# A fused decoder layer on one core: the output projection of five token tiles moved from the mixer into the attention, by way of DRAM

## What is computed

```python
# block 1, the mixer: a state space layer on layernorm(x)
zxbcdt = x @ W_in.T                      # z 1024, xBC 1280, dt 64 columns
xBC = silu(causal_conv(xBC)); dt = softplus(dt_raw + dt_bias)
M = (C @ B.T) * exp(cum_i - cum_j) * dt  # per head, chunks of 128 tokens
y = M @ xs + exp(cum) * C @ S_prev + D * xs
yz = y * silu(z)
yn = yz * rsqrt(mean(yz * yz) + EPS) * norm_w
x = x + yn @ W_out.T                     # 1024 -> 512, the output projection
# block 2: softmax attention of layernorm(x) over the context, 32 query heads, 8 kv heads of 16
# block 3: the two best of 8 gated experts for each token
```

## Time and profile before

| | |
|---|---|
| median of 3 runs | 1400.34 us (1399.75 to 1400.81) |
| the profiled execution's own time | 1394.34 us |
| its span, first to last instruction | 1392.4 us |
| mean granted TensorE clock | 0.977 of full |
| busy share PE, PEld, DVE, ACT, POOL | 92, 53, 59, 51, 42% |
| instructions | 23244 |

### The profile page before, as it was taken

The page is one execution under the profiler, slowest core; times in us unless marked ns, Lnnn a source line. Parts: engine busy times, 40 slices in busy tenths (PEclk is TensorE's granted clock), DMA queues, the critical chain, the costliest instruction groups (busy, mean ns, idle before and its releaser), DMA issues.

```text
span 1392.4 us, 23244 instructions
## 1 busy us (share of the span) xinstructions
PE 1286.9 (92%) x7783; PEld 739.6 (53%) x7783; DVE 822.8 (59%) x1840; ACT 705.9 (51%) x1350; POOL 580.8 (42%) x871
## 2 busy tenths in 40 slices
PE   6799999999999999888888888889999999999996
PEld 4567777767676767553334334234444444444443
DVE  5898888787878778578988898661111111111111
ACT  2767676777767666744778767641111111111110
POOL 1465556665656556672333334341222222222221
PEclk9999999999999999987999999989999999999999
DMA  9000000000000000002001010023344344344222
GB/s 351 24 8 5 8 6 9 5 8 5 8 6 8 5 4 9 9 1 102 13 28 44 32 32 33 32 77 106 77 137 136 58 133 143 80 103 136 46 46 31
DMA packets 40354, 73.41 MB, mean 53 GB/s; under 512 B 18544, under 2 KB 22896, under 8 KB 39216
## 3 DMA queue, kind: packets, MB, share of 16 engines
q1 hardware_dynamic: 30304, 48.49, 10.0%
q0 software_dynamic: 8736, 20.61, 7.9%
q10 hardware_dynamic: 1200, 2.82, 0.5%
HBM read 149.30 MB, written 19.99 MB: 122 GB/s over the span
## 4 chain that ended last, share of the span: by engine, by line
PE 66%; DVE 18%; issue 6%; ACT 5%; POOL 3%; DMA 1%; SPq 1%; POOLq 0%; DVEq 0%; ACTq 0%
PE work_ps L572 12%; PE gate_ps L1573 10%; PE up_ps L1573 10%; PE down_ps L1557 9%; PE work_ps L644 7%; PE work_ps L577 4%; DVE maxes L1263 3%; DVE conv L771 3%; PE work_ps L1089 3%; PE mturn_ps L577 2%; DVE decay L767 2%; PE work_ps L664 2%; PE work_ps L1080 2%; ACT prob L1161 1%; PE work_ps L652 1%
## 5 line engine op out<-in xcount | busy, mean ns | idle before, releaser
L572 PE MATMUL work_ps<-xnT,w_in 128*128 128x256 f32 (+1 forms) x1216 | 289.1, 386 | 4.3 <-DVE xdt L902 2.4
L572 PEld LDWEIGHTS work_ps<-xnT,w_in 128*128 128x128 f32 (+1 forms) x1216 | 226.8, 193 | 54.8 <-issue 21.9
L767 POOL TENSOR_TENSOR decay<-decay,cbm 128x512 f32<-128x512 f32 x128 | 183.8, 1437 | 147.4 <-ACT decay L762 144.3
L1661 POOL DMA_INDIRECT out_dram<-y_out,ids x39 | 61.9, 1587 | 334.3 <-DVE row_w L1625 228.7
L1263 DVE TENSOR_REDUCE maxes<-work_ps 128x2 f32<-128x512 f32 x256 | 166.0, 681 | 28.7 <-PE work_ps L1065 27.7
L1161 ACT ACTIVATE prob<-work_ps 128x512 f32<-128x512 f32 x256 | 142.3, 609 | 66.2 <-PE work_ps L1080 65.6
L1640 DVE TENSOR_TENSOR act<-gelu,up_ps 128x512 f32<-128x512 f32 x39 | 26.8, 688 | 251.8 <-PE up_ps L1573 251.8
L762 ACT ACTIVATE decay<-decay 128x512 f32<-128x512 f32 x256 | 162.1, 640 | 12.5 <-DVE xnT L1212 5.4
L758 ACT ACTIVATE decay<-work_ps 128x512 f32<-128x512 f32 x256 | 138.7, 600 | 38.4 <-PE work_ps L652 37.8
L1573 PE MATMUL gate_ps<-w_e,xgT 128*128 x312 | 140.5, 593 | 1.4 <-ACT xgT L1590 1.0
L1557 PE MATMUL down_ps<-w_e,actT 128*128 x312 | 140.4, 593 | 0.8 <-ACT actT L1603 0.8
(11 more groups left out here) (271 smaller groups left out, 1947.7 us busy)
## 6 DMA issues: line engine op xcount, KB each, us to landing
w_e<-c_experts_dram SPq DMA_DIRECT2D x39, 3072.0 KB
normed_tokens<-r_xn SPq DMA_DIRECT2D x17, 256.0 KB, 2.2
out_dram<-x_sb SPq DMA_DIRECT2D x17, 256.0 KB, 2.5
x_sb<-x_dram SPq DMA_DIRECT2D x1, 3072.0 KB, 17.4
w_in<-c_w_inT_dram ACTq DMA_DIRECT2D x1, 2560.0 KB, 11.8
w_in<-c_w_inT_dram SPq DMA_DIRECT2D x1, 2048.0 KB, 9.7
w_out<-c_w_outT_dram SPq DMA_DIRECT2D x1, 2048.0 KB, 22.5
RT<-cum_scratch SPq DMA_DIRECT2D x32, 48.0 KB
```

Source lines behind the costliest of these rows:

```text
L572: m = e.matmul(ps[0:width, at:at + L], w_in[:, k, col:col + width], xnT[b % 2][:, k, :], start=(k == 0), stop=(k == KD - 1))
L767: return e.tensor_tensor(four(decay[s % NDECAY]), four(decay[s % NDECAY]), cb, ALU.mult)
```

## The change

LATE names tiles 7, 9, 11, 13 and 15, the second tiles of sequences 3 to 7. For these the mixer makes the gated rows and their sum of squares, root included, as before, but in place of `out` and `x_add` SyncE stores the rows (512 KB) to DRAM (`yz_out`, slot f + 9), and the rows' buffer is free once the store has landed. In the attention SyncE loads them back (`yz_in`) and TensorE does `out` in 8 parts of one matmul (two records): tile 7 at items 1, 3, ... 15 with x_add at 17, its load in slot -1 behind `mixed` and `n_out(0, 1)` of slot -2; tile 9 at items 25, 28, ... 46 with x_add at 48, its load at item 20; the others 32 items later each. `yz_in` of tile 9 to 15 waits for `out` of the tile before in the list. Late `out` takes one of the five shared banks from its first part to x_add.

The rows of roots are kept per tile (y_rows for rstats). `mixed` waits for `rstat` of the last tile. The query statistics of sequences 0 and 1 stay together; those of 2 to 7 are made one sequence at a time, two `q_bn` at items 2 and 3 of each 32, `q_stats` at 4, `q_newton` at 5. The small routing tables are loaded at item 2 as before, the first expert's weights at item 162, after `out` of tile 15. The buffers of w_out, yz and some small ones change places in memory, so that w_out and yz stay alive in the attention.

The diff, without the lines that only change a buffer's place:

```diff
@@ -42,6 +42,8 @@
 BANKS = 8
+LATE = [TPB * b + 1 for b in range(3, NB)]
+OUT_PARTS = lambda tile: 8 if tile in LATE else 4
 DT_COL, X_COL = HID, HID + NH
@@ -140,7 +142,10 @@
             put(f + 13, ("rms_newton", tile))
-            for part in range(4):
+            if tile in LATE:
+                put(f + 9, ("yz_out", tile))
+                continue
+            for part in range(OUT_PARTS(tile)):
                 put(f + 9 + part, ("out", tile, part))
@@ -186,7 +191,7 @@
     return slots
-DMA_ONLY = {"freed", "mixed", "cum_out", "cum_in", "ctx_in", "n_out", "router_in", "first_expert", "r_store", "out_in", "c_weight_out", "keep_warm", "warm"}
+DMA_ONLY = {"yz_out", "yz_in", "freed", "mixed", "cum_out", "cum_in", "ctx_in", "n_out", "router_in", "routing_in", "first_expert", "r_store", "out_in", "c_weight_out", "keep_warm", "warm"}
 
@@ -230,6 +235,8 @@
     def allowed(stage, *key):
+        if stage == "out" and key[0] in LATE:
+            return range(5)
         if stage == "score":
@@ -262,11 +269,11 @@
             put(r - 12, ("ctx_in", b))
-        if b and b % 2 == 0:
-            for t in range(2 * TPB):
-                put(r + t, ("q_bn", b * TPB + t))
-            put(r + 4, ("q_stats", b // 2))
-            put(r + 5, *[("q_newton", b // 2, i) for i in range(3)])
+        if b >= 2:
+            for t in range(TPB):
+                put(r + 2 + t, ("q_bn", b * TPB + t))
+            put(r + 4, ("q_stats", b))
+            put(r + 5, *[("q_newton", b, i) for i in range(3)])
         for t in range(TPB):
@@ -286,7 +293,8 @@
         if b == 1:
-            put(2, ("first_expert",))
+            put(2, ("routing_in",))
+            put(n * 5 + 2, ("first_expert",))
         for g in range(4):
@@ -305,6 +313,12 @@
             put(f + 20 + late + 2 * t, ("r_keep", b, t))
+    for m, tile in enumerate(LATE):
+        at, step = (n * m - 7, 3) if m else (1, 2)
+        put(at - 5 if m else -1, ("yz_in", tile))
+        for part in range(OUT_PARTS(tile)):
+            put(at + step * part, ("out", tile, part))
+        put(at + step * 7 + 2, ("x_add", tile))
     for g, at in enumerate((4 * n + 20, 7 * n, 7 * n + 27)):
@@ -355,6 +369,7 @@
     tokens = nc.dram_tensor("normed_tokens", [(NT + 1) * P, DIM + NE], F32).ap()
+    yz_dram = nc.dram_tensor("yz_scratch", [len(LATE), P, HID], F32).ap()
     cum_dram = [nc.dram_tensor(f"cum_scratch{i}", [3, NH, TPB, P], BF16).ap() for i in range(2)]
@@ -379,6 +394,7 @@
         store_weights = semaphore("store_weights")
+        store_yz, load_yz = semaphore("store_yz"), semaphore("load_yz")
         load_e = [semaphore(f"load_e{i}") for i in range(WR)]
@@ -395,6 +411,7 @@
         a_rows = sb(top, "a_rows", [P, 4, NT])
+        y_rows = sb(top, "y_rows", [P, 4, NT])
         xnT = [sb(top, "xnT0", [P, KD, L])]
@@ -405,9 +422,12 @@
...
+            yz = [sb(st, f"yz{i}", [P, NCZ, P]) for i in range(2)]
...
@@ -637,10 +654,14 @@
                 if part == 0:
-                    e.wait_ge(*done("yz", tile // TPB, tile % TPB, 1))
+                    if tile in LATE:
+                        e.wait_ge(load_yz, 16 * (LATE.index(tile) + 1))
+                    else:
+                        e.wait_ge(*done("yz", tile // TPB, tile % TPB, 1))
                     if tile == 0:
                         e.wait_ge(*done("scale_out"))
-                for ct in (2 * part, 2 * part + 1):
+                each = NCZ // OUT_PARTS(tile)
+                for ct in range(each * part, each * (part + 1)):
                     m = e.matmul(work(stage, tile)[:, :], yz[tile % 2][:, ct, :], w_out[:, ct, :], start=(ct == 0), stop=(ct == NCZ - 1))
@@ -914,27 +935,31 @@
                 if tile >= 2 and hf == 0:
-                    e.wait_ge(*done("out", tile - 2, 3))
+                    if tile - 2 in LATE:
+                        e.wait_ge(store_yz, 16 * (LATE.index(tile - 2) + 1))
+                    else:
+                        e.wait_ge(*done("out", tile - 2, OUT_PARTS(tile - 2) - 1))
                 own.settle(e.tensor_tensor(y, four(dx), four(work("y", b, c, hf)), ALU.add))
...
                 e.wait_ge(*done("ones", b, c, hf))
+                now = slice(b * TPB + c, b * TPB + c + 1)
                 if hf == 0:
-                    e.tensor_copy(rstats[:, 3:4], work("ones", b, c, hf)[:, 0:1]).then_inc(piece_done[stage], 1)
+                    e.tensor_copy(y_rows[:, 3, now], work("ones", b, c, hf)[:, 0:1]).then_inc(piece_done[stage], 1)
                 else:
-                    e.tensor_tensor(rstats[:, 0:1], work("ones", b, c, hf)[:, 0:1], rstats[:, 3:4], ALU.add).then_inc(piece_done[stage], 1)
+                    e.tensor_tensor(y_rows[:, 0, now], work("ones", b, c, hf)[:, 0:1], y_rows[:, 3, now], ALU.add).then_inc(piece_done[stage], 1)
             elif stage == "rms":
...
                 e.wait_ge(*done("rstat", tile // TPB, tile % TPB, 1))
-                own.settle(e.tensor_scalar(rstats[:, 0:1], rstats[:, 0:1], 0.25 / HID, RMS_EPS, ALU.mult, ALU.add))
-                root_guess(e, own, rstats[:, 0:1], rstats[:, 1:2], rstats[:, 2:3]).then_inc(piece_done[stage], 1)
+                own.settle(e.tensor_scalar(y_rows[:, 0, tile:tile + 1], y_rows[:, 0, tile:tile + 1], 0.25 / HID, RMS_EPS, ALU.mult, ALU.add))
+                root_guess(e, own, *[y_rows[:, i, tile:tile + 1] for i in range(3)]).then_inc(piece_done[stage], 1)
             elif stage == "x_add":
...
                 e.wait_ge(*done("rms_newton", tile))
-                e.wait_ge(*done("out", tile, 3))
-                e.scalar_tensor_tensor(x_sb[:, tile, :], work("out", tile)[:, :], rstats[:, 1:2], x_sb[:, tile, :], ALU.mult, ALU.add).then_inc(piece_done[stage], 1)
+                e.wait_ge(*done("out", tile, OUT_PARTS(tile) - 1))
+                e.scalar_tensor_tensor(x_sb[:, tile, :], work("out", tile)[:, :], y_rows[:, 1, tile:tile + 1], x_sb[:, tile, :], ALU.mult, ALU.add).then_inc(piece_done[stage], 1)
             elif stage == "mix_v":
@@ -981,7 +1006,7 @@
                 e.wait_ge(*done("rms", *key))
-                root_newton(e, own, rstats[:, 0:1], rstats[:, 1:2], rstats[:, 2:3]).then_inc(piece_done[stage], 1)
+                root_newton(e, own, *[y_rows[:, i, key[0]:key[0] + 1] for i in range(3)]).then_inc(piece_done[stage], 1)
 
@@ -1023,6 +1048,11 @@
 
+            elif stage == "yz_out":
+                tile, = key
+                e.wait_ge(*done("yz", tile // TPB, tile % TPB, 1))
+                e.dma_start(yz_dram[LATE.index(tile), :, :], yz[tile % 2][:, :, :].rearrange("p c j -> p (c j)")).then_inc(store_yz, 16)
+
         def repeated(e, bank, count):
@@ -1040,7 +1070,7 @@
             elif stage == "mixed":
-                e.wait_ge(*done("x_add", NT - 1))
+                e.wait_ge(*done("rstat", *last_unit))
             elif stage == "k_turn":
@@ -1135,7 +1165,7 @@
                 tile = b * TPB + t
-                e.wait_ge(*done("q_newton", b // 2, 2))
+                e.wait_ge(*done("q_newton", b if b >= 2 else 0, 2))
                 if b:
@@ -1234,15 +1264,16 @@
                 tile, = key
-                if tile >= 2 * TPB and tile % (2 * TPB) == 0:
-                    e.wait_ge(*done("q_stats", tile // (2 * TPB) - 1))
+                if tile >= 2 * TPB and tile % TPB == 0:
+                    e.wait_ge(*done("q_stats", tile // TPB - 2 if tile >= 4 * TPB else 0))
+                if tile in LATE:
+                    e.wait_ge(*done("x_add", tile))
                 e.bn_stats(a_bn[:, tile % (2 * TPB), :], x_sb[:, tile, :]).then_inc(piece_done[stage], 1)
             elif stage == "q_stats":
-                j, = key
-                ts = slice(2 * TPB * j, 2 * TPB * (j + 1))
+                ts = queried(*key)
                 e.wait_ge(*done("q_bn", ts.stop - 1))
-                for t in range(2 * TPB):
-                    m = e.bn_aggr(a_mv[:, ts.start + t, :], a_bn[:, t, :])
+                for t in range(ts.start, ts.stop):
+                    m = e.bn_aggr(a_mv[:, t, :], a_bn[:, t % (2 * TPB), :])
                 own.settle(m)
@@ -1401,6 +1432,9 @@
 
+        def queried(j):
+            return slice(TPB * j, TPB * (j + 1)) if j else slice(0, 2 * TPB)
+
         def placed_in(t):
@@ -1423,10 +1457,10 @@
             elif stage == "mixed":
-                e.wait_ge(*done("x_add", NT - 1))
+                e.wait_ge(*done("rstat", *last_unit))
             elif stage == "q_newton":
                 j, step = key
-                ts = slice(2 * TPB * j, 2 * TPB * (j + 1))
+                ts = queried(j)
                 e.wait_ge(*(done("q_newton", j, step - 1) if step else done("q_stats", j)))
@@ -1492,11 +1526,19 @@
                 e.wait_ge(load_ctx, 16 * (b + 1))
-            elif stage == "first_expert":
+            elif stage == "yz_in":
+                tile, = key
+                e.wait_ge(store_yz, 16 * len(LATE))
+                if tile - 2 in LATE:
+                    e.wait_ge(*done("out", tile - 2, OUT_PARTS(tile - 2) - 1))
```

(6 more changed lines are left out.)

13 lines of the change are left out of this document (6 added, 7 removed).

## The result

The changed kernel takes 1411.45 us (median of 8 runs, 1404.91 to 1414.71), the kernel before 1400.03 in the same comparison (8 runs). The ratio is **1.0087, 95% interval 1.0064 to 1.0109**: 12 us slower, where 4 us faster was forecast, and 1.4 us above the range given.

The account below looks back on a forecast made before the run. TensorE, busy 92%, nearly fills the mixer; in the attention no engine is full and they wait in turns. Mixer -18.1, first scores net 0, start +5, tiles 9 to 15 +9: -4.1, so 1396 us against 1400.34, range 1382 to 1410.

Parts of the forecast that it names:

- Mixer, 18.1: Mixer batches of tiles 7 to 13: 20.1 us gained without the late projection, less 2 for the clock, so 18.1.
- x_add and its wait and the 0.90 go: 4.1 us: Steady mixer, tiles 7 and 9: VectorE loses x_add, its wait and a z gate wait, 4.1 us gained per tile.
- The mixer's end, 6: Mixer's end, tile 15: without its groups VectorE's queue decides and the first score comes 6 us earlier.
- the 6 gained are waited away: Attention's start: tile 7's rows load in 3.3 us and later work queues behind, so the net gain is 0.
- The start, 5: Attention's first items, to item 16: tile 7's parts and half clock cost 0.6 to 5.6 us, 5 taken.
- Tiles 9 to 15, 9: Attention items 25 to 142: four tiles' parts cost 9 us, between TensorE's own sum of 5.9 and full exposure of 27.6.
- a part fits behind two waiting scores: Attention, tiles 9 to 15: a part of 0.86 us fits there, the reason for taking 9 us, near the low end.
- they go with the uncertainty of the 9: Query statistics by batch: three more small chains, 0.5 us on VectorE and 3.3 on POOL, given no cost of their own.
- SyncE's wait for yz holds only transfers due ten slots later: Mixer's yz stores: SyncE's wait for yz delays nothing needed soon, so it costs nothing.
- B: Rival: the attention absorbs the parts, 0 to 5.9 in place of 9; 11.6 to 27 us faster, 1373 to 1389; chance 0.18.
- D: Rival: with four shared banks left, TensorE's waits for folds double, 23 in place of 9; 1410 us, slower; chance 0.25.
- C: Rival: the attention's start eats the rest, half clock through item 24, 9 in place of 5; 1400 us, no change; chance 0.19.

Follow-up runs that it names:

- floor: Changed kernel without the late tiles' projection: no matmuls, bank, yz load or x_add; yz stores and statistics by batch stay; 1384.27 us, 0.9892 against the kernel before.
- the run with three late tiles: Kernel before with only tiles 11, 13 and 15 projected among the attention's items, tile 15 from its own buffer, statistics in twos; 1403.15 us, ratio 1.0006.
- the statistics alone: Kernel before with only the query statistics and Newton steps made batch by batch from batch 2 on, late tiles kept in the mixer; 1411.04 us, ratio 1.0044.
- the Newton steps early: Changed kernel with the query statistics of batches 3 to 7 put 12 items earlier; 1410.99 us, ratio 1.0054 to the kernel before.
- runs with less work: Changed kernel with six of eight matmuls per late tile 16 columns wide, 1413.92 us, or left out with their weight loads, 1407.33 us.
- repairs: Changed kernel with tile 7's projection from item 6, statistics of batches 3 to 7 twelve items earlier, yz loads of tiles 9 to 15 five items earlier; together 1408.33 us.
- the doubled ones: Changed kernel with seven of eight matmuls of each late tile issued twice: 1433.04 us, ratio 1.0236; with the three repairs as well 1435.33 us, 1.0254.
- both cut: Changed kernel with six of eight matmuls of each late tile left out and the three repairs; 1392.57 us, ratio 0.9948 to the kernel before.

## Why the prediction was wrong

The sum was -18.1 (mixer), -6 (first scores), +6 (waited away at the yz load), +5 (half clock), +9 (tiles 9 to 15), statistics within the 9. Set against the runs:

| step | forecast | measured |
|---|---|---|
| up to the first score | -24.1 | -17.9 (traces) |
| statistics by batch | in the 9 | +2.8 (floor less the line above, a ratio less a trace) to +6.2 (alone) |
| projection among the items, start included | +20 | +27.3 (changed kernel less floor) |
| sum | -4.1 | +12.2 |

**Mixer, 18.1: too large.** From tile 7's yz to tile 15's it was 288.8 us before and is 275.8 now: 13.1 gained. The step that failed is "x_add and its wait and the 0.90 go: 4.1 us" for tiles 7 and 9, which gave 2.9 and 2.6. VectorE in time, changed kernel, where the earlier trace rows has the wait of 0.90:

```profile
429.52 0.69 DVE L896 SCALAR_TENSOR_TENSOR zs<-zs,work_ps 128x512 f32<-128x512 f32 x1 [1.57 <-ACT zs L754]
```

The wait for ScalarE's z gate did not go, it grew to 1.57: VectorE came earlier, ScalarE did not. That VectorE and not TensorE decides was right: from this gate to the yz behind it is 14.91 us in both kernels. Tile 11's batch gave 2.3 for 5.6; the one behind it, tile 13's, 5.3 for 6.3. For tile 11 the forecast leaned on the whole shift of a wait by 5.2 us, and what ended that batch instead stays open.

**The mixer's end, 6: right.** From tile 15's yz to the first score 18.0 us became 11.1, 6.9 gained; the remaining 2 us between this and the 17.9 were lost before tile 7, at the run's start, where nothing was changed in the work.

**The yz load, "the 6 gained are waited away": right** in place and size: a gap of 5.67 us, the load 3.5 us where 3.3 was taken (the page's issues of both kinds):

```profile
yz_scratch<-yz SPq DMA_DIRECT2D x5, 512.0 KB, 2.6
yz<-yz_scratch SPq DMA_DIRECT2D x5, 512.0 KB, 3.5
```

The Trainium skill (DMA: Bandwidth & Descriptors, the chain of events with its two cost components) gives some 3.2 us by its figures, an estimate, as they are for transfers that GpSimd issues and SyncE issues here; the trace is 0.3 above it.

**The start, 5: too large.** The clock was at half behind the gap, as said, though only to 638. Wait and clock were to cost 6 + 5 = 11. From the first exponent to the 24th it is 8.4 us more than in the kernel before, and 10.2 more than without the late projection, tile 7's parts included. Not all of it can be got back, since item 6 is not free either.

**Tiles 9 to 15, 9: the largest miss.** 27.3 less some 9 for the start leaves 18, four tiles at the 5.3 of the run with three late tiles would be 21, and the traces have 16.2 from the 24th to the 144th exponent (145.1 against 128.9 without the late projection): inside the bounds of 5.9 and 27.6, but about twice the value taken. Two things in that step were wrong. A part was priced at 0.86 us, a quarter of a group of four in a row; alone between other work it takes 1.05 to 1.10 in the chain, 8.5 a tile in place of 6.9. And "a part fits behind two waiting scores" took idle time of TensorE over 22 items for room. At every third item a tile costs 4.1 (traces) to 5.3 (three late tiles), with parts at successive items 3.1 more, up to these eight parts in full. So waiting scores hide a third to a half of the work, not the two thirds on which the 9 rested (9 of 27.6).

**Statistics, "they go with the uncertainty of the 9": wrong.** This was the named edit costed at nothing. GpSimd's 40% load said nothing of whose way the 3.8 us of Newton steps would stand in; the wait was one step on, at VectorE's r_stats. Behind the last late tile, from the 144th exponent on, the changed kernel takes 7.8 us more than the one before, the statistics alone 9.8, and the changed kernel with the Newton steps early 2.5.

**The loop through the SP queue was not seen at all.** "SyncE's wait for yz holds only transfers due ten slots later" looked at what stands behind the yz transfer. What stands ahead of the load, the stores of r_xn and a context load that SyncE waits for, put it on the path. It fits what the runs show, that neither bound gives its price when removed alone. The clock, lower in the runs with less work and without repairs (0.93 and 0.96 from 680 to 800 us), can have a part in that, and no run separates it.

**The rivals.** B (the attention absorbs the parts) was wrong by the run without them, 27.3 us faster than the changed kernel, and by the doubled ones. By the busy share of weight loads, which the Trainium skill (Perfetto Trace Analysis, identifying the most-contended engine) puts above matmul busy time, TensorE has as much room after as before: 92.97 us of 245 against 92.55, 38%. The trace does not bear that out: at 38% added matmuls are paid for, in full once doubled. D foresaw the right time, 1410, by the wrong mechanism: waits for folds fell from 24.1 to 12.7 us, and the chance given to it was for a bank. C, the start alone, was too small a cause: half clock ended at 638. The Trainium skill (Perfetto Trace Analysis, optimization strategy) advises interleaving phases whose busiest engine differs; here both phases lean on TensorE, and only tile 15 gained by it.

Of the signs set out: batches with a late tile last 68.6 to 68.8 us, not 67; the first score came at 626.4, where -24.1 would give 620.3; the gap was there; the attention took 307 us, over the 290 that was named as showing the 5 and the 9 wrong. Two of the signs did not fit the sum they stood for: "near 638" left out the mixer's gain, and 272 with 6, 5 and 9 on it is 292, outside the 278 to 290 named as right.

## What to carry to other kernels

Before work is moved onto an engine, take its price from its smallest piece standing alone (1.06 us here, 0.86 in a row), and count idle time as room only where a queue of ready work stands on both sides of the piece; double the moved work in a trial, since here the doubled run showed the full price where removal uncovered the next bound. Measure a piece from its start to the next start: by the durations of its records a cut of 22 us looked like a small one. When removing a suspect brings too little, follow the chain of that run: a second loop of nearly the same length (38.5 us a batch here) can hide behind the first, so that only with both cut either shows its worth. Of a small step moved into more batches ask not how busy its engine is but what stands behind it there and who waits for that.

## What was not expected of the hardware

A 128x16 f32 matmul record with its own weight load took 284 ns in the mean against 638 for one of 512 columns, and a matmul of two such records 0.33 us from start to next start against 1.06: thirty-two times fewer columns, two thirds of the time gone. The run that made six of eight matmuls so narrow had the lower mean clock, 0.952 against 0.966, and was as slow as the full work. The runs don't separate what the clock and the second loop each took of it. Of the clock's course: with 5.67 us of gap and half clock around it (0.63 and 0.59 in the windows 600 to 625 and 625 to 640), it was full again from 638 on, while in the kernel before it was 0.55 until 656 after smaller gaps; so the size of one gap did not tell how long the half clock lasted.
